# Deep attention in 32-query tiles, sixteen heads a step, with another order of the deep queues

## The reference

```python
for i in range(DEPTH):
    x = attn_layer(shift_tokens(x), Wqkv[i], q_scale[i], k_scale[i], Wo[i]) + x
    x = ffn_layer(shift_tokens(x), ln_g[i], ln_b[i], W1[i], b1[i], W2[i], b2[i]) + x
```

```python
bk2, bv2 = look(bk), look(bv)          # (previous window, own window): 64 keys for 32 queries
mask = (it < jb) | (it > jb + w) | (jb == -1)
sim = jnp.einsum('bhwie,bhwje->bhwij', bq, bk2) * QK_SCALE
attn = jax.nn.softmax(jnp.where(mask, -jnp.finfo(sim.dtype).max, sim), -1)
out = jnp.einsum('bhwij,bhwje->bhwie', attn, bv2)
```

## Time and profile before

| what | value |
|---|---|
| median of three runs | 3415.38 us (3412.5 to 3415.92) |
| profiled execution, span | 3416.1 us |
| PE busy | 3315.1 us (97%) |
| weight loads (PEld) busy | 2569.2 us (75%) |
| DVE busy | 3131.4 us (92%) |
| ACT busy | 3070.7 us (90%) |
| POOL busy | 2754.7 us (81%) |
| mean granted TensorE clock | 0.991 of full speed |

### The profile page before, as it was taken

The page is one execution under the profiler, slowest core; times in us unless marked ns, Lnnn a source line. Parts: engine busy times, 40 slices in busy tenths (PEclk is TensorE's granted clock), DMA queues, the critical chain, the costliest instruction groups (busy, mean ns, idle before and its releaser), DMA issues.

```text
span 3416.1 us, 108621 instructions
## 1 busy us (share of the span) xinstructions
PE 3315.1 (97%) x42631; PEld 2569.2 (75%) x43104; DVE 3131.4 (92%) x4801; ACT 3070.7 (90%) x5393; POOL 2754.7 (81%) x2749
## 2 busy tenths in 40 slices
PE   8998799999999999999999999999999999999997
PEld 6885577777777777777777777777777777777776
DVE  6886899999999999999999999999999999999994
ACT  5665799999999999999999999999999999999996
POOL 3433888888889888988988888898898888888882
PEclk9998999999999999999999999999999999999999
DMA  1000222122112212212211221222122222122111
GB/s 45 28 3 29 58 56 59 41 63 57 48 47 59 53 51 57 56 44 54 68 46 47 56 59 40 68 53 50 47 59 53 54 53 53 39 74 53 45 44 43
DMA packets 61706, 171.35 MB, mean 50 GB/s; under 512 B 9488, under 2 KB 21392, under 8 KB 60816
## 3 DMA queue, kind: packets, MB, share of 16 engines
q1 hardware_dynamic: 61200, 164.36, 19.1%
HBM read 21.72 MB, written 4.19 MB: 8 GB/s over the span
## 4 chain that ended last, share of the span: by engine, by line
PE 92%; DVE 3%; issue 3%; ACT 1%; POOL 1%; POOLq 0%; DVEq 0%; ACTq 0%
PE bank L969 11%; PE bank L1021 11%; PE bank L1037 10%; PE bank L1002 9%; PE bank L921 9%; PE bank L986 9%; PE bank L1361 7%; PE bank L922 7%; PE bank L920 4%; PE bank L1374 3%; PE bank L380 2%; PE bank L360 2%; PE bank L1346 2%; PE bank L345 2%; PE bank L1336 1%
## 5 line engine op out<-in xcount | busy, mean ns | idle before, releaser
L1286 POOL TENSOR_TENSOR rotbuf<-mbuf 128x512 f32<-128x512 f32 x768 | 971.5, 1276 | 319.7 <-PE bank L969 298.1
L1300 POOL TENSOR_TENSOR rotbuf<-rotbuf,rs 128x512 f32<-128x512 f32 x768 | 792.3, 1049 | 7.5
L1310 POOL TENSOR_TENSOR probs<-probs,rden 128x768 f32<-128x768 f32 x384 | 561.1, 1472 | 23.6 <-DVE rden L1252 23.6
L1063 ACT ACTIVATE sq<-bank 128x512 f32<-128x512 f32 x768 | 456.7, 595 | 100.6 <-PE bank L922 89.6
L1173 DVE TENSOR_TENSOR mbuf<-bank,table 128x512 f32<-128x512 f32 x768 | 519.2, 676 | 21.6 <-ACT sq L1063 15.8
L1174 DVE TENSOR_TENSOR mbuf<-bank,table 128x512 f32<-128x512 f32 x768 | 522.5, 680 | 0.0
L921 PE MATMUL bank<-weights,inputs 128*128 128x512 bf16 x1152 | 440.1, 382 | 40.8 <-issue 14.7
L969 PE MATMUL bank<-ident,rotbuf 128*128 128x128 f32 x3072 | 460.1, 281 | 6.5 <-DVE mbuf L1174 5.3
L1155 DVE TENSOR_REDUCE ss<-sq 128x16 f32<-128x1024 f32 x384 | 463.6, 1207 | 0.0
L1021 PEld LDWEIGHTS bank<-probs_t,vbuf 96*64 96x64 f32 x12288 | 389.5, 138 | 85.0 <-issue 57.2
L1021 PE MATMUL bank<-probs_t,vbuf 96*64 96x64 f32 x12288 | 442.5, 225 | 4.2 <-ACT probs_t L1128 3.9
(11 more groups left out here) (116 smaller groups left out, 6259.3 us busy)
## 6 DMA issues: line engine op xcount, KB each, us to landing
vbuf<-v_stage SPq DMA_DIRECT2D x192, 384.0 KB, 4.4
vbuf<-v_stage SPq DMA_DIRECT2D x192, 256.0 KB, 3.5
vbuf<-v_stage SPq DMA_DIRECT2D x96, 128.0 KB, 4.3
stage<-in_wqkv SPq DMA_DIRECT2D x36, 256.0 KB, 4.8
weights<-in_wo SPq DMA_DIRECT2D x6, 512.0 KB, 6.2
out_t<-weights SPq DMA_DIRECT2D x1, 2048.0 KB, 6.3
weights<-out_t SPq DMA_DIRECT2D x1, 2048.0 KB, 10.6
out_t<-weights SPq DMA_DIRECT2D x16, 128.0 KB, 2.2
```

Source lines behind the costliest of these rows:

```text
L1286: e.tensor_tensor(b.rot[:, u, :], b.m1[:, u % 2, :], b.m2[:, u % 2, :], ALU.add).then_inc(s.rotated, 1)
L1300: e.tensor_tensor(v, v, r, ALU.mult).then_inc(s.scaled, 1)
L1310: e.tensor_tensor(probs, probs, b.rden[:, p % 2, :].unsqueeze(2).broadcast_to([P, 8, BLOCK_K]), ALU.mult).then_inc(s.probs, 1)
```

## The change

1. Tiles. A score tile is 32 queries by exactly its 64 keys. A step `t` of the softmax takes 128 queries and all 16 heads: 16 x 64 = 1024 columns, in two steps instead of four. Mask, scores, max, shift, exp, sum, reciprocal, normalise and `act_copy_out` run twice per instance. The transposes of probabilities and the value products run in four sub-steps `i`, each with 4 transposes of 128 x 128 and 32 value products of 64 rows, 64 wide, 32 columns. `act_copy_pt_of` copies 128 x 512.
2. PE positions. The 64 score products of a step go to 2 x 4 positions of the array (64 rows by 32 columns of weights), where there were 16 products at 2 x 2 positions. The value products go to 2 x 2 positions, where each took all rows at 2 positions.
3. Values. Each 32-query tile has its own 64 values in `b.v`, twice: heads of one half on partitions 0 to 63, of the other on 64 to 127. This takes 18 DMAs of 512 columns instead of 5 of 1024. The host permutes the value columns of the weights.
4. Banks. Bank 5 alone takes transposed probabilities, and banks 6 and 7 take the output. `pe_write_banks` writes both score banks once before the deep block, and the first mask waits for it.
5. Order. All five deep queues, `WORK_RING` and the reaches are new. The first layer does the same work in buffers at other places.

```diff
-PLACED = (48, 32)
-PV_EXTRA = 6
+SPAN_K = 2 * WINDOW
+STEPS = 2
+SUBS = 4
+SLOTS = HEADS // 2
+PLACED = (160, 128)
...
-STAGE_FROM, SPLIT_FROM, LATE_AT, OUTER_AT = 0, 2, 11, 4
+STAGE_FROM, SPLIT_FROM, LATE_AT, OUTER_AT = 0, 3, 11, 4
...
+def pe_write_banks(e, s, b):
...
+    for parity in range(2):
+        mm = e.matmul(b.scores[parity][:, :], b.inv_dim[:, :], b.X[:, 0:512], start=True, stop=True, skip_group_check=True)
+    mm.then_inc(s.banks_written, 1)
...
+def pe_scores_of(e, s, b, at, ahead, t):
...
+    e.wait_ge(s.masked, k.c[STEPS] + (t + 1))
+    e.wait_ge(s.t_copied, k.c[8] + (4 * t + 4))
+    for slot in range(SLOTS):
+        for quarter in range(4):
+            for parity in range(2):
+                r = slice(64 * parity, 64 * parity + 64)
+                first = P * t + WINDOW * quarter
+                mm = e.matmul(b.scores[parity][32 * quarter:32 * quarter + 32, SPAN_K * slot:SPAN_K * (slot + 1)],
+                              b.q[r, slot, first:first + WINDOW], b.k[r, k.par, slot, first:first + SPAN_K],
+                              start=False, stop=slot == SLOTS - 1, skip_group_check=True)
+    mm.then_inc(s.scores, 1)
...
+    for j in range(2):
+        for quarter in range(4):
+            for odd, parity in ((0, 0), (1, 1), (0, 1), (1, 0)):
+                r, out_r = slice(64 * odd, 64 * odd + 64), slice(64 * parity, 64 * parity + 64)
+                value = DIM_HEAD * (4 * half + 2 * j + parity)
+                prob = P * (2 * parity + j) + WINDOW * quarter
+                out = P * (2 * half + j) + WINDOW * quarter
+                mm = e.matmul(b.outs[odd][out_r, out:out + WINDOW], b.v[r, k.par, 4 * t + quarter, value:value + DIM_HEAD],
+                              b.deep_ptf[r, i % 2, prob:prob + WINDOW], start=True, stop=True)
...
+def sp_place_values(e, s, b, at, ahead):
...
+    e.wait_ge(s.pv_full, k.c[SUBS] - SUBS)
+    for odd in range(2):
+        r, col = 64 * odd, slice(512 * odd, 512 * (odd + 1))
+        e.wait_ge(s.v_copied, k.c[4] + (odd + 1))
+        e.dma_start(b.v[r + 32:r + 64, k.par, 0, :], b.vstage[0:32, 0, col]).then_inc(s.v_placed[0], 16)
+        e.dma_start(b.v[r:r + 64, k.par, 1, :], b.vstage[0:64, 0, col]).then_inc(s.v_placed[0], 16)
+        e.dma_start(b.v[r:r + 64, k.par, 2, :], b.vstage[32:96, 0, col]).then_inc(s.v_placed[0], 16)
+        e.dma_start(b.v[r:r + 64, k.par, 3, :], b.vstage[64:128, 0, col]).then_inc(s.v_placed[0], 16)
+        e.dma_start(b.v[r:r + 32, k.par, 4, :], b.vstage[96:128, 0, col]).then_inc(s.v_placed[0], 16)
...
+    pe_project_in(e, s, b, at, 2, 6)
+    pe_values_of(e, s, b, at, 0, 0)
+    pe_transpose(e, s, b, at, 1, 5)
+    pe_values_in(e, s, b, at, 2, 0)
+    pe_transpose_probs_of(e, s, b, at, 0, 2)
+    pe_project_in(e, s, b, at, 2, 7)
...
+    pe_ff_mean(e, s, b, at, -1)
+    pe_scores_of(e, s, b, at, 1, 0)
+    pe_values_in(e, s, b, at, 2, 1)
+    pe_transpose_probs_of(e, s, b, at, 0, 3)
...
+    pe_project_in(e, s, b, at, 3, 1)
+    pe_project_in(e, s, b, at, 3, 2)
+    pe_project_in(e, s, b, at, 3, 3)
+    pe_values_of(e, s, b, at, 0, 3)
+    pe_scores_of(e, s, b, at, 1, 1)
+    pe_transpose(e, s, b, at, 2, 2)
+    pe_values_in(e, s, b, at, 2, 3)
+    pe_transpose_probs_of(e, s, b, at, 1, 0)
...
 def sp_deep_slot(e, s, b, at):
 
     sp_place_values(e, s, b, at, 1)
-    sp_next_weights(e, s, b, at(1))
+    sp_next_weights(e, s, b, at(3))
```

More of the change, by code:

```diff
@@ L380, in pe_first_values @@
                 mm = e.matmul(b.out[row:row + 32, P * t + BLOCK_Q * half:P * t + BLOCK_Q * (half + 1)],
-                              b.v[:, k.par, 2 * t + half, P * j + row:P * j + row + 32],
-                              b.deep_ptf[:, p % 2, col:col + BLOCK_Q], start=j == 0, stop=j == 3)
+                              b.v0[:, k.par, 2 * t + half, P * j + row:P * j + row + 32],
+                              b.first_ptf[:, p % 2, col:col + BLOCK_Q], start=j == 0, stop=j == 3)
     mm.then_inc(s.pv_full, 1)
@@ L977, in pe_scores_of, with pe_transpose_probs_of @@
         return
[L978 to L987, removed]
-                          b.k[r, k.par, slot, BLOCK_Q * blk:BLOCK_Q * blk + BLOCK_K], start=False, stop=j == 3,
-                          skip_group_check=True)
+    e.wait_ge(s.masked, k.c[STEPS] + (t + 1))
[8 more added lines that the diff above has]
+                              start=False, stop=slot == SLOTS - 1, skip_group_check=True)
     mm.then_inc(s.scores, 1)
-def pe_transpose_probs_of(e, s, b, at, ahead, p):
+def pe_transpose_probs_of(e, s, b, at, ahead, i):
     k = at(ahead)
@@ L997, in pe_transpose_probs_of, with pe_values_of @@
         return
-    e.wait_ge(s.probs, k.c[4] + (p + 1))
-    e.wait_ge(s.pt_copied, k.c[4] + p)
+    t, half = divmod(i, 2)
+    e.wait_ge(s.probs, k.c[STEPS] + (t + 1))
+    e.wait_ge(s.pt_copied, k.c[SUBS] + i)
     for parity in range(2):
-        for j in range(4):
-            mm = e.transpose(b.pt[parity][0:BLOCK_K, P * j:P * (j + 1)], b.deep_probs[:, p % 2, 4 * parity + j, :], b.ident[:, :])
+        for j in range(2):
+            slot = SLOTS * parity + 4 * half + 2 * j
+            place = P * (2 * parity + j)
+            mm = e.transpose(b.pt_deep[:, place:place + P], b.probs[:, t, slot:slot + 2, :].rearrange("p h k -> p (h k)"), b.ident[:, :])
     mm.then_inc(s.pt_full, 1)
-def pe_values_of(e, s, b, at, ahead, p):
+def pe_values_of(e, s, b, at, ahead, i):
     k = at(ahead)
@@ L1010, in pe_values_of @@
         return
-    t, half = divmod(p, 2)
-    e.wait_ge(s.pt_copied, k.c[4] + (p + 1))
-    e.wait_ge(s.out_copied, k.c[4] + p)
+    t, half = divmod(i, 2)
+    e.wait_ge(s.pt_copied, k.c[SUBS] + (i + 1))
     if half == 0:
+        e.wait_ge(s.out_copied, k.c[STEPS] + t)
         e.wait_ge(s.v_placed[t], k.c[PLACED[t]] + PLACED[t])
-    for j in range(4):
-        for blk_half in range(2):
-            for parity in range(2):
-                h, r = 8 * half + 2 * j + parity, slice(64 * parity, 64 * parity + 64)
-                col = P * j + BLOCK_Q * blk_half
-                mm = e.matmul(b.out[r, col:col + BLOCK_Q], b.v[:, k.par, 2 * t + blk_half, DIM_HEAD * h:DIM_HEAD * (h + 1)],
-                              b.deep_ptf[:, p % 2, 512 * parity + col:512 * parity + col + BLOCK_Q], start=True, stop=True)
+    for j in range(2):
+        for quarter in range(4):
[6 more added lines that the diff above has]
+                              b.deep_ptf[r, i % 2, prob:prob + WINDOW], start=True, stop=True)
     mm.then_inc(s.pv_full, 1)
@@ L1977 @@
     x = arr(L0_attn_x)
+    wqkv = arr(L0_ffn_Wqkv)
+    of_head = [2 * (2 * group + odd) + parity for odd in range(2) for group in range(SLOTS // 2) for parity in range(2)]
+    values = wqkv[:, :, 2 * INNER:].reshape(DEPTH, DIM, HEADS, DIM_HEAD)[:, :, of_head].reshape(DEPTH, DIM, INNER)
+    wqkv = np.concatenate([wqkv[:, :, :2 * INNER], values], 2)
     bq = arr(L0_attn_b_qkv)
```

367 lines of the change are left out of this document (169 added, 198 removed), and 8 rows, old and new, of the table WORK_RING.

## The result

The changed kernel takes 3308.57 us (median of 4 runs, 3304.44 to 3316.18) against 3415.65 us of the kernel before on the same chip. The ratio is 0.9691, with a 95% interval of 0.9679 to 0.9704: 107 us less, where 278 less were forecast. The sign is right and the time lies in the range, but at its far end. The question is where the other 170 us went.

A forecast was written before the change was run, and what follows sets the result against it. PE was taken as the bound: 3.03 us less per slot over 96 slots is 291, plus 3, minus 1.7, so 292 off 3416.1 gives 3124, or 3138 us with waits. Range 3095 to 3310 us.

The forecast's parts named there:

- Transposes: On PE, 32 transposes of probabilities per slot become 16 at 0.109 us each, saving 1.74 us a slot.
- Value groups: On PE, weight loads set the pace, so halving moving columns changes nothing: 1.08 us a group, 4.32 a slot.
- rival (d): Weight loads hidden behind matmuls in the values: 1.8 us a slot less on PE, DVE bounds, 2946 us; chance 0.04.
- rival (b): Score products run four positions abreast instead of eight: 1.8 us a slot more, 3310 us; chance 0.09.
- durations of all changed operations on DVE, ACT and POOL: Fewer, wider operations save 4.5 us a slot on DVE, 4.2 on ACT, 2.1 on POOL; all need at most 26.7.
- The placements: 18 value DMA issues take 10.8 us of SP's 28.5 per slot; with 2 us margin they cost nothing.
- Rival (c): A MATMUL with its load starts no faster than every 21 ns: slot 33.7 us, 3620 us, slower; chance 0.07.
- the rule of the Trainium skill: Matmul starts never under about 25 ns apart: some 7 us more per slot, kernel over 400 us slower; prediction rejected it.
- the term of the scores: On PE, 16 rounds at eight positions: two score steps cost 2.12 us against 3.32, 1.20 less a slot.
- rival (a): PE stalls on its new order or late instruction packets: 0.7 to 1.5 us a slot, 3190 to 3270 us; chance 0.18.
- 0.15 us a slot for all waits: Allowance for waits of the new order, about half of what was unassigned in the old slot; raises 3124 to 3138 us.

The follow-up runs named there:

- run with small transfers: Changed kernel with each of the 18 placement DMAs moving 64 of its 512 columns, values mostly missing: 3298.66 us, ratio 0.9651.
- half-columns experiment: Changed kernel with all 64 score products per step kept, each taking 32 keys instead of 64: 3295.5 us, ratio 0.9642.
- half-instructions experiment: Changed kernel with 32 score products of 128 columns per step instead of 64 of 64, scores not the reference's: 3155.79 us, ratio 0.9233.
- score step in two halves: Changed kernel with each score step split around the mean or an input projection, and values (0,3) behind transposes (2,2): 3401.99 us, ratio 0.9956.
- value group moved: Changed kernel with value group (0,3) moved from directly ahead of scores (1,1) to between projections (3,1) and (3,2): 3255.71 us, ratio 0.9521.
- score step later: Changed kernel with scores (1,1) moved behind transposes (2,2) and the three bf16 products that follow: 3342.11 us, ratio 0.9782.
- value group moved further: Changed kernel with value group (0,3) moved ahead of all three projections before scores (1,1): 3303.66 us, ratio 0.9655.

## Why the prediction was right in sign and wrong in size

**Right.** PE bounded the kernel and still does; no engine took its place. Transposes cost 0.44 us a group of four. Value groups cost 1.06 us with 32 moving columns, where 1.08 was taken: their rounds of 58 ns depend neither on the moving columns nor, at 14.6 ns per MATMUL, on the pace of instructions found above. That leaves the weight load, as the prediction had it, though no run varied it alone; rival (d) is refuted. Eight positions run abreast, so rival (b) is refuted too. The durations of all changed operations on DVE, ACT and POOL came within 7%. The placements cost at most the 10 us that the run with small transfers gave back. Rival (c), an even pace of 21 ns per MATMUL, is refuted by the 8.3 ns. With it goes the rule of the Trainium skill, page "TensorE: Matmul & The Clock Gate", section "Wait — 56ns, not 53.3ns?", that starts are never less than about 25 ns apart: it is not a floor across positions, where MATMULs start 7 ns apart. (The price that the prediction gives for it, over 400 us more than before, does not follow from its own terms: 7 us a slot less the 3.03 saved are 4 us, some 380 in 96 slots.)

**Wrong, first: the term of the scores.** The prediction took "16 rounds of 64 columns with weights 32 wide, which is exactly the first layer's value group", 1.06 us. The columns are the same and so are the rounds, but a round there has two MATMULs and here eight. I had priced the pace of issue only as a rival at 21 ns, an upper bound from groups in which the array sets the pace; below it I put nothing in the sum. The trace of before could not give the true figure, since its fastest rounds are four MATMULs each. Measured: 1.42 and 1.48 us, 0.78 more per slot. The first 64 instructions run at the array's pace, as if they had been collected while the work before them ran (that they were is not shown; that it is the count that matters, the half-columns experiment shows); then each MATMUL with its load costs 8.3 ns at best, 67 ns for a round that the array could do in 56. The half-columns experiment shows the same 67 ns with less to stream, the half-instructions experiment rounds that do not slow down. Here the Trainium skill, page "TensorE: Matmul & The Clock Gate", section "Measured speedup vs the span model", gives about 4 ns of issue per tile; with the load counted as an instruction of its own the trace agrees at best, 8.3 ns for two, and its mean of 10.7 is above. By that rule with loads counted a step has 256 x 4 = 1.02 us of issue beside 1.06 of rounds, an estimate that would have shown how near the two are.

**Wrong, second: rival (a) left out of the sum.** The sum held 0.15 us a slot for all waits, and 1.2 us of stops are measured. The rival had the mechanism, "empties one in 0.9 us, faster than one engine refills it", and a price of 0.7 to 1.5 us a slot, but a chance of 0.18. (The 0.9 us itself was too short, as the first point says: at the measured pace 256 instructions take 1.4 us.) Its estimate of a packet was good: the changed kernel has 45,198 instructions and 179 packets more than the kernel before, 252 to a packet, and the half-instructions kernel 24,576 and 96 fewer, 256. In the slot the value group (0,3) and the scores (1,1) behind it are 384 PE instructions in about 2.5 us, one and a half packets, with a packet taking 1.09 us and PE going on 1.2 to 1.6 us after it has landed. The mean slot lies 1.5 us above the shortest in the window (30.59 and 29.09), and the stops make 80 us over 65 slots, 1.2 us each. What spoke for the rival stood in the prediction already: instructions per score step, time per packet. The trace of before has no such stop; but its longest burst is a value group with a score group behind it, 128 instructions, so that it said nothing on 384.

**The account.** The half-instructions kernel has a shortest slot of 28.36 us, with score groups of 1.09. Groups of 1.42 and 1.48 add 0.72: 29.08, and the changed kernel has 29.09. Of the 1.5 us from there to its mean in the window 1.2 are the 57 stops, of which the six for POOL and DVE make 0.14. What is left, about 0.3 us a slot, was not divided further; the shorter waits of the transposes for POOL are a small part of it. Over the whole run the mean slots of the two kernels are 30.21 and 28.66 us, and 96 times their difference of 1.55 is 149 of the 153 us between them. The missing 170 us are these 153 and the 17 by which the half-instructions kernel is itself above 3138. In the window its slot is 28.85 us where the forecast with its allowance had 28.70, and 96 times that difference is 14 of the 17.

**Open.** What holds the first 64 instructions of a group, how far ahead of PE the packets are taken, and why it goes on only some 1.3 us after the end of the packet, no run here shows. That the packets cause the stops rests on their place in time and on the kernels in which fewer instructions in a row made them rarer: of stops for "issue" over 0.55 us there were 51, and there are none with half the score instructions, 11 with the score step in two halves, 20 with the value group moved, 27 with the score step later and 17 with the value group moved further. No run changed the delivery of packets alone. Tiles of 32 queries with the old order of the queues were not tried.

**The best version.** The kernel with the value group moved, 3255.71 us, beats both; it takes 0.9521 of the time before.

## What to carry to other kernels

When matmuls are cut into smaller tiles that run abreast, count instructions beside columns: here a MATMUL with its load needs, after the first 32, 8.3 ns at best and 10.7 on average, so eight abreast with 64 columns are already paced by their instructions, and the four abreast of the value groups (16.6 ns per MATMUL) are not. Then count the instructions that stand in a row: 384 of them were stopped, for some 1.2 us at a time, in about every second slot, and one independent group moved away more than halved the stops for instructions. Such a move must be followed to the other queues: three others also spaced out the instructions, two lost more at a mask or a work bank than they gained, and the third came out about even, 5 us below the changed kernel.

## What was not expected of the hardware

- A group of eight positions runs at two paces: 56 ns a round for the first 32 MATMULs and 32 loads (80 for the first step), and then 67 ns, with steps of up to 147 ns between. The change comes behind 32 MATMULs also with rounds of 128 and of 32 columns.
- PE can be stopped for 1.35 us in the middle of a group with data and semaphores ready, and goes on 1.2 to 1.6 us after a 16 KB packet of instructions (1.09 us) has ended.
- That packet's duration depends little on other traffic: 1.09 us at a DMA share of 0.29, 0.99 at 0.07.
- With weights 64 wide, a value group takes 1.06 us with 32 moving columns and 1.08 with 64.
